# Recurrence of two GRU layers: the half-precision state cast on ScalarE, candidate sums in PSUM, keep's high products last

## The chip, the cores and the metric

The kernel runs on one core of a Trainium2 chip. The metric is the time of one execution on the device in microseconds (us), median of three runs. A core has five engines that matter here, each with its own queue worked off in order: TensorE (PE; its weight loads are listed as PEld), VectorE (DVE), ScalarE (ACT), GpSimd (POOL) and SyncE (SP, which issues DMAs). They meet only through semaphores.

## The reference

Four layers over x of shape (8, 16, 16, 96): a spectral block, a Toeplitz block, and two blocks that are the same function with other weights. Each of those two normalises x, projects it, and runs four GRUs over the 256 positions (two directions for each of two weight sets), then gates and projects back. What matters is the GRU step:

```python
def step(hprev, gxt):
    gh = hprev @ whh.T + bhh
    r = jax.nn.sigmoid(gxt[:, :h] + gh[:, :h])
    z = jax.nn.sigmoid(gxt[:, h:2 * h] + gh[:, h:2 * h])
    n = jnp.tanh(gxt[:, 2 * h:] + r * gh[:, 2 * h:])
    hn = (1.0 - z) * n + z * hprev
    return (hn, hn)
```

The batch is 8 and h is 96. The 256 steps of a layer can't be reordered, as each takes the state of the step before.

## The kernel before

The program runs the layers one after the other. `gru_steps` holds the recurrence of one layer and is called twice (tensor names L2s_... and L3s_...). The four GRUs are two groups of two: group g handles its two GRUs with 8 batch rows each, PER = 16 columns on 96 partitions. The groups don't depend on each other. Every engine's queue treats group 0, then group 1, of step q, then goes on to q + 1, so while one group waits for an engine the other can use it.

The state is kept in fp32 (`states`, all 257 of them), and for the products as two half-precision parts: `h_hi`, the state rounded, and `h_lo`, what is left. Weights are in two half-precision parts too. In PSUM lie the sums of three gates, 8 steps (STEPS) to a chunk and two chunks deep: reset and keep (r and z) and cand (n). The input's share is added ahead of time by products of 64 columns (8 rows by 8 steps, L1161) for the next chunk, `ahead(gate, first)`: six for each gate and group, spread over the steps from `first` on. The hidden state's share (L1185, 8 columns each) is per group and step: for each gate four "high" products (two weight parts, two GRUs) with h_hi, and two "low" ones with h_lo. Sums of a chunk that was used are zeroed by ScalarE (L1135, L1137) at two steps of a chunk.

One step of a group, engine by engine:

- TensorE waits for h_hi (L1193), adds the high products of reset, cand and keep, then input products for reset, waits for h_lo (L1205), adds low reset (releases the reset sigmoid), low cand, input products for keep, low keep (releases the keep sigmoid), input products for cand.
- ScalarE: reset sigmoid (L1128), keep sigmoid (L1130), renew = sigmoid of the negated keep sum (L1131), then tanh of the candidate (L1133).
- VectorE: `candidate` (L1063), `kept_part` (L1070, keep times old state), `new_state` and `rest` (L1085, h_lo = state - h_hi). Multiply-and-add of two tensors is done by a scan over interleaved pairs of 32 elements for 16 results: with pairs (0, a) and (k, b) it gives k * a + b at the odd places. `new_state` issues the scan twice: once with half-precision output into h_hi (L1077), once in fp32 into `states` (L1079).

VectorE's order over both groups is written out by hand:

```python
candidate(0, q); rest(1, q - 1); kept_part(0, q); new_state(0, q)
candidate(1, q); rest(0, q);     kept_part(1, q); new_state(1, q)
```

(two lines here for eight in the kernel). From the middle of a layer on GpSimd adds forward and backward states into `y` (L1112), four operations each time 8 steps are complete.

Of the kernel before, what the change touches and what calls it, by code (L numbers as in the profile page):

```python
# [27 lines left out]
ALU = mybir.AluOpType  # L28
ACT = mybir.ActivationFunctionType

P = 128
BATCH, SIDE, C = 8, 16, 96
# [35 lines left out]
PER = 2 * BATCH  # L68


def flat(ap):

    return ap.rearrange("p a b -> p (a b)")
# [921 lines left out]
def gru_steps(nc, layer, weights, forward, states, y):  # L995
# [8 lines left out]
    with ExitStack() as ctx:  # L1004
# [3 lines left out]
        each = lambda n: [sem(f"{n}{g}") for g in range(GROUPS)]  # L1008
        bank = lambda n: ctx.enter_context(nc.psum_tensor(f"{layer}s_{n}", [P, 4, PER, STEPS], F32))
        reset = pairs("reset", [C, 2, PER, 2])  # L1010
        cand = pairs("cand", [C, 2, PER, 2])
        keep = pairs("keep", [C, 2, PER])
        renew = pairs("renew", [C, 2, PER, 2])
        terms = pairs("terms", [C, 2, PER, 2])
# [7 lines left out]
        reset_sum = lambda g, p: reset_bank[g][:, p]  # L1022
        keep_sum = lambda g, p: keep_bank[g][:, p]
        cand_sum = lambda g, p: cand_bank[g][p][:, 0:2].rearrange("p a c s -> p (a c) s").rearrange("p (c k) s -> p c k s", k=2)
        warm = sb("warm", [C, 1])
        prepared = sem("prepared")

# [10 lines left out]
        with nc.Block() as block:  # L1038

            @block.vector  # L1040
            def _(e):
# [16 lines left out]
                def candidate(g, q):  # L1058

                    p, s = q // STEPS % 2, q % STEPS  # L1060
                    x = q % 2
                    e.wait_ge(advanced[g], 5 * q + 2)
                    e.tensor_tensor_scan(flat(cand[g][:, x]), flat(reset[g][:, x]), flat(cand_sum(g, p)[0:C, :, :, s]), 0.0,  # L1063
                                         ALU.mult, ALU.add).then_inc(cand_ready[g], 1)

                def kept_part(g, q):
# [6 lines left out]
                def new_state(g, q):  # L1073

                    x = q % 2
                    e.wait_ge(advanced[g], 5 * q + 5)
                    e.tensor_tensor_scan(flat(h_hi[g][0:C, x]), flat(renew[g][:, x]), flat(terms[g][:, x]), 0.0,  # L1077
                                         ALU.mult, ALU.add).then_inc(hi_ready[g], 1)
                    e.tensor_tensor_scan(flat(states[g][:, q + 1]), flat(renew[g][:, x]), flat(terms[g][:, x]), 0.0,  # L1079
                                         ALU.mult, ALU.add).then_inc(updated[g], 1)  # L1080

                def rest(g, q):

                    e.wait_ge(updated[g], q + 1 + BEFORE[g])
                    e.tensor_tensor(h_lo[g][:, q % 2], states[g][:, q + 1, :, 1], h_hi[g][0:C, q % 2, :, 1],  # L1085
                                    ALU.subtract).then_inc(lo_ready[g], 1)

# [27 lines left out]
            @block.scalar  # L1115
            def _(e):

                e.wait_ge(prepared, 1)
                e.activation(warm[:], warm[:], ACT.Sigmoid)
                e.wait_ge(prepared, PREPARED)  # L1120
                for q in range(SEQ):
                    p, s = q // STEPS % 2, q % STEPS
                    x = q % 2
                    renewed = 1 <= q // STEPS < CHUNK_COUNT - 1
                    for g in range(GROUPS):

                        e.wait_ge(reset_summed[g], q + 1)
                        e.activation(reset[g][:, x, :, 1], reset_sum(g, p)[0:C, :, s], ACT.Sigmoid).then_inc(advanced[g], 1)  # L1128
                        e.wait_ge(keep_summed[g], q + 1)
                        e.activation(keep[g][:, x], keep_sum(g, p)[0:C, :, s], ACT.Sigmoid).then_inc(advanced[g], 1)  # L1130
                        e.activation(renew[g][:, x, :, 1], keep_sum(g, p)[0:C, :, s], ACT.Sigmoid, scale=-1.0)  # L1131
                        e.wait_ge(cand_ready[g], q + 1)
                        e.activation(terms[g][:, x, :, 0], cand[g][:, x, :, 1], ACT.Tanh).then_inc(advanced[g], 1)  # L1133
                        if renewed and s == RESET_ZEROED:
                            e.activation(reset_sum(g, 1 - p)[0:C], zeros[:], ACT.Copy).then_inc(zeroed[g], 1)  # L1135
                        if renewed and s == KEEP_ZEROED:
                            e.activation(keep_sum(g, 1 - p)[0:C], zeros[:], ACT.Copy).then_inc(zeroed[g], 1)  # L1137

            @block.tensor
            def _(e):  # L1140
# [34 lines left out]
                for q in range(SEQ):  # L1175
# [3 lines left out]
                    for g in range(GROUPS):  # L1179
# [14 lines left out]

                        before, at = divmod(q - 1, STEPS)
                        zeroing = 1 <= before < CHUNK_COUNT - 1 and at in (RESET_ZEROED, KEEP_ZEROED)
                        for gate in (CAND, KEEP, RESET) if zeroing and at == RESET_ZEROED else (RESET, CAND, KEEP):
                            if zeroing and gate == (RESET if at == RESET_ZEROED else KEEP):
                                e.wait_ge(zeroed[g], 2 * (before - 1) + (1 if at == RESET_ZEROED else 2))
                            for j in range(2):  # L1200
                                add(gate, 0, 0, j)
                                add(gate, 1, 0, j)
                        ahead(RESET, RESET_ZEROED + 1)

                        e.wait_ge(lo_ready[g], q + 1)  # L1205
# [1 line left out]
                        add(RESET, 0, 1, 1).then_inc(reset_summed[g], 1)  # L1207
                        add(CAND, 0, 1, 0)
                        add(CAND, 0, 1, 1).then_inc(advanced[g], 1)
                        ahead(KEEP, KEEP_ZEROED + 1)  # L1210
                        add(KEEP, 0, 1, 0)
                        add(KEEP, 0, 1, 1).then_inc(keep_summed[g], 1)
# [186 lines left out]
```

## Time and profile before

| | |
|---|---|
| median of 3 runs | 1206.0 us (1205.65 to 1208.2) |
| the profiled execution | 1204.91 us |
| its span in the profile | 1203.1 us |
| busy TensorE / VectorE / ScalarE / GpSimd | 1085.8 / 950.9 / 773.5 / 154.9 us |
| granted TensorE clock, mean | 0.583 of full speed |
| DMA over the span | 12.59 MB |

Times of rows are from the start of the span. A matmul's end is modelled, so its start is what tells; a group of alike matmuls in a row is shown as one line with the start of the first. The time of an instruction that follows directly on another overlaps it.

### The profile page before, as it was taken

What the parts mean: (1) busy time and instruction counts of PE and PEld (TensorE: products, weight loads), DVE (VectorE), ACT (ScalarE), POOL (GpSimd) and SP (SyncE); (2) the same over time, 40 slices, a digit from 0 to 9 for tenths busy, and PEclk for the clock granted to TensorE, in tenths of its full rate; (3) what the DMA queues carried; (4) which work ended last, traced back from release to release, by engine and by line L of the source; (5) the groups of instructions that cost most, each with busy time, mean ns of one, the idle gap of its engine ahead of it and who ended that gap; (6) DMA issues with size and microseconds to landing.
All of it is one profiled execution on the core that took longest, in us unless ns stands there. A gap on an engine that the chain in (4) does not pass through costs nothing. (4 is left out here: it accounts for less than half of the span.)

```text
span 1203.1 us, 55551 instructions
## 1 busy us (share of the span) xinstructions
PE 1085.8 (90%) x22424; PEld 860.0 (71%) x22424; DVE 950.9 (79%) x5703; ACT 773.5 (64%) x4503; POOL 154.9 (13%) x222
## 2 busy tenths in 40 slices
PE   3787799958999999999999989999999999999997
PEld 2554344445888888888888866788888888888886
DVE  3544699987888888888888876788888888888884
ACT  4223530007788788777777773788788777777773
POOL 1001379920000000001000100000000001000100
PEclk9587899957555555555555556555555555555555
DMA  4000500000000000000000000000000000000000
GB/s 121 2 1 12 133 1 1 1 0 7 4 4 4 4 4 4 4 4 4 4 4 4 3 4 5 4 4 3 4 4 4 4 3 4 4 4 4 4 4 27
DMA packets 8220, 12.59 MB, mean 10 GB/s; under 512 B 5746, under 2 KB 7122, under 8 KB 7675
## 3 DMA queue, kind: packets, MB, share of 16 engines
q1 hardware_dynamic: 7962, 9.05, 3.0%
q8 instruction: 175, 2.87, 1.0%
q14 instruction: 83, 0.67, 0.2%
HBM read 8.26 MB, written 0.79 MB: 8 GB/s over the span
## 5 line engine op out<-in xcount | busy, mean ns | idle before, releaser
L1077 DVE TENSOR_TENSOR_SCAN L3s_h_hi<-L3s_renew,L3s_terms 96x32 f16<-96x32 f32 x512 | 114.5, 224 | 64.3
L1077 DVE TENSOR_TENSOR_SCAN L2s_h_hi<-L2s_renew,L2s_terms 96x32 f16<-96x32 f32 x512 | 114.5, 224 | 64.2
L1185 PE MATMUL L3s_reset_sum<-L3s_h_hi,L_w_hidden 97*128 97x8 f16 x2048 | 139.6, 179 | 11.6 <-DVEq L1054 0.4
L1185 PE MATMUL L2s_reset_sum<-L2s_h_hi,L_w_hidden 97*128 97x8 f16 x2048 | 139.6, 179 | 11.6 <-DVEq L1054 0.4
L1112 POOL TENSOR_TENSOR L_y<-L_states 96x64 f32<-96x64 f32 x128 | 40.9, 355 | 843.1 <-DVE L_states L1079 843.1
L1185 PEld LDWEIGHTS L3s_reset_sum<-L3s_h_hi,L_w_hidden 97*128 97x128 f16 x2048 | 94.4, 107 | 62.1 <-DVE L3s_h_hi L1077 13.8
L1185 PEld LDWEIGHTS L2s_reset_sum<-L2s_h_hi,L_w_hidden 97*128 97x128 f16 x2048 | 94.4, 107 | 62.1 <-DVE L2s_h_hi L1077 13.8
L1133 ACT ACTIVATE L3s_terms<-L3s_cand 96x16 f32<-96x16 f32 x512 | 111.5, 218 | 37.5 <-DVE L3s_cand L1063 6.0
L1133 ACT ACTIVATE L2s_terms<-L2s_cand 96x16 f32<-96x16 f32 x512 | 111.5, 218 | 37.4 <-DVE L2s_cand L1063 5.9
L1185 PE MATMUL L3s_cand_sum<-L3s_h_hi,L_w_hidden 97*128 97x8 f16 x2048 | 131.3, 175 | 4.5 <-DVE L3s_h_hi L1077 3.1
L1185 PE MATMUL L2s_cand_sum<-L2s_h_hi,L_w_hidden 97*128 97x8 f16 x2048 | 131.3, 175 | 4.5 <-DVE L2s_h_hi L1077 3.1
L1185 PE MATMUL L3s_keep_sum<-L3s_h_hi,L_w_hidden 97*128 97x8 f16 x2048 | 130.0, 174 | 0.0
L1185 PE MATMUL L2s_keep_sum<-L2s_h_hi,L_w_hidden 97*128 97x8 f16 x2048 | 130.0, 174 | 0.0
L1128 ACT ACTIVATE L3s_reset<-L3s_reset_sum 96x16 f32<-96x16 f32 x512 | 93.0, 182 | 53.2 <-PE L3s_reset_sum L1185 1.1
L1128 ACT ACTIVATE L2s_reset<-L2s_reset_sum 96x16 f32<-96x16 f32 x512 | 93.0, 182 | 53.2 <-PE L2s_reset_sum L1185 1.0
L1185 PE MATMUL L3s_reset_sum<-L3s_h_lo,L_w_hidden 96*128 96x8 f16 x1024 | 114.1, 185 | 0.5 <-DVE L3s_h_lo L1085 0.2
L1185 PE MATMUL L2s_reset_sum<-L2s_h_lo,L_w_hidden 96*128 96x8 f16 x1024 | 114.0, 185 | 0.4 <-DVE L2s_h_lo L1085 0.2
L1185 PE MATMUL L3s_keep_sum<-L3s_h_lo,L_w_hidden 96*128 96x8 f16 x1024 | 112.1, 183 | 0.0
L1185 PE MATMUL L2s_keep_sum<-L2s_h_lo,L_w_hidden 96*128 96x8 f16 x1024 | 112.1, 183 | 0.0
L1063 DVE TENSOR_TENSOR_SCAN L3s_cand<-L3s_reset,L3s_cand_sum 96x32 f32<-96x32 f32 x512 | 110.4, 216 | 2.0 <-ACT L3s_reset L1128 1.1
L1063 DVE TENSOR_TENSOR_SCAN L2s_cand<-L2s_reset,L2s_cand_sum 96x32 f32<-96x32 f32 x512 | 110.4, 216 | 2.0 <-ACT L2s_reset L1128 1.1
L692 DVE SCALAR_TENSOR_TENSOR l_acc<-l_v,coef,l_acc 96x384 f32<-96x384 f32 (+11 forms) x88 | 103.6, 1241 | 0.4
(257 smaller groups left out, 3517.9 us busy)
## 6 DMA issues: line engine op xcount, KB each, us to landing
L_wih_raw<-in_L_wih SPq DMA_DIRECT2D x2, 1152.0 KB, 11.4
l_w_raw<-in_L_w SPq DMA_DIRECT2D x1, 1296.0 KB
L_w_hidden_raw<-in_L_whh SPq DMA_DIRECT2D x2, 576.0 KB
stream<-in_x SPq DMA_DIRECT2D x2, 384.0 KB, 3.8
out<-stream SPq DMA_DIRECT2D x4, 192.0 KB, 2.1
l_idft<-in_idft SPq DMA_DIRECT2D x1, 400.0 KB
rpe_lw<-in_rpe_lw SPq DMA_DIRECT2D x1, 384.0 KB
l_dft<-in_dft SPq DMA_DIRECT2D x1, 288.0 KB, 2.9
```

The source lines that it names most:

```text
L692: e.scalar_tensor_tensor(out=row(to, acc), in0=row(of, v), scalar=coef[:, m, axis, at:at + 1], in1=row(to, acc), op0=ALU.mult, op1=ALU.add ...
L1063: e.tensor_tensor_scan(flat(cand[g][:, x]), flat(reset[g][:, x]), flat(cand_sum(g, p)[0:C, :, :, s]), 0.0, ALU.mult, ALU.add).then_inc(can ...
L1077: e.tensor_tensor_scan(flat(h_hi[g][0:C, x]), flat(renew[g][:, x]), flat(terms[g][:, x]), 0.0, ALU.mult, ALU.add).then_inc(hi_ready[g], 1)
L1112: e.tensor_tensor(y[:, m, :, t:t + STEPS].rearrange("p b t -> p t b"), hist[g0][:, t:t + STEPS, j0, :], mirrored, ALU.add)
L1128: e.activation(reset[g][:, x, :, 1], reset_sum(g, p)[0:C, :, s], ACT.Sigmoid).then_inc(advanced[g], 1)
L1133: e.activation(terms[g][:, x, :, 0], cand[g][:, x, :, 1], ACT.Tanh).then_inc(advanced[g], 1)
L1185: return e.matmul(dst, weights.hidden[0:rows, wp, GATES * (2 * g + j) + gate, :], rhs, start=False, stop=False, skip_group_check=True)
```

## The change

ScalarE makes h_hi: a copy of the finished fp32 state with half-precision output, `high_half`, issued between the other group's reset sigmoid and keep sigmoid. VectorE's half-precision scan goes. `rest` now waits for h_hi (`hi_ready`) in place of the state (`updated`). The candidate scan writes its 32 results into unused columns of the bank of its own cand sums in PSUM, where tanh reads them, and no longer into SBUF. On TensorE, keep's four high products move from before the wait for h_lo to after the low products of reset and cand; a wait for a zeroed bank stays with its gate. Number and shape of the products are unchanged.

```diff
--- before.py
+++ after.py
@@ -1008,7 +1008,6 @@
         each = lambda n: [sem(f"{n}{g}") for g in range(GROUPS)]
         bank = lambda n: ctx.enter_context(nc.psum_tensor(f"{layer}s_{n}", [P, 4, PER, STEPS], F32))
         reset = pairs("reset", [C, 2, PER, 2])
-        cand = pairs("cand", [C, 2, PER, 2])
         keep = pairs("keep", [C, 2, PER])
         renew = pairs("renew", [C, 2, PER, 2])
         terms = pairs("terms", [C, 2, PER, 2])
@@ -1022,6 +1021,8 @@
         reset_sum = lambda g, p: reset_bank[g][:, p]
         keep_sum = lambda g, p: keep_bank[g][:, p]
         cand_sum = lambda g, p: cand_bank[g][p][:, 0:2].rearrange("p a c s -> p (a c) s").rearrange("p (c k) s -> p c k s", k=2)
+
+        cand = lambda g, p, x: cand_bank[g][p][0:C, 2].rearrange("p c s -> p (c s)")[:, x * 2 * PER:(x + 1) * 2 * PER]
         warm = sb("warm", [C, 1])
         prepared = sem("prepared")
 
@@ -1060,7 +1061,7 @@
                     p, s = q // STEPS % 2, q % STEPS
                     x = q % 2
                     e.wait_ge(advanced[g], 5 * q + 2)
-                    e.tensor_tensor_scan(flat(cand[g][:, x]), flat(reset[g][:, x]), flat(cand_sum(g, p)[0:C, :, :, s]), 0.0,
+                    e.tensor_tensor_scan(cand(g, p, x), flat(reset[g][:, x]), flat(cand_sum(g, p)[0:C, :, :, s]), 0.0,
                                          ALU.mult, ALU.add).then_inc(cand_ready[g], 1)
 
                 def kept_part(g, q):
@@ -1074,14 +1075,12 @@
 
                     x = q % 2
                     e.wait_ge(advanced[g], 5 * q + 5)
-                    e.tensor_tensor_scan(flat(h_hi[g][0:C, x]), flat(renew[g][:, x]), flat(terms[g][:, x]), 0.0,
-                                         ALU.mult, ALU.add).then_inc(hi_ready[g], 1)
                     e.tensor_tensor_scan(flat(states[g][:, q + 1]), flat(renew[g][:, x]), flat(terms[g][:, x]), 0.0,
                                          ALU.mult, ALU.add).then_inc(updated[g], 1)
 
                 def rest(g, q):
 
-                    e.wait_ge(updated[g], q + 1 + BEFORE[g])
+                    e.wait_ge(hi_ready[g], q + 2)
                     e.tensor_tensor(h_lo[g][:, q % 2], states[g][:, q + 1, :, 1], h_hi[g][0:C, q % 2, :, 1],
                                     ALU.subtract).then_inc(lo_ready[g], 1)
 
@@ -1122,15 +1121,22 @@
                     p, s = q // STEPS % 2, q % STEPS
                     x = q % 2
                     renewed = 1 <= q // STEPS < CHUNK_COUNT - 1
+
+                    def high_half(g, q):
+                        e.wait_ge(updated[g], q + 1 + (0, 1)[g])
+                        e.activation(h_hi[g][0:C, q % 2, :, 1], states[g][:, q + 1, :, 1], ACT.Copy).then_inc(hi_ready[g], 1)
+
                     for g in range(GROUPS):
 
                         e.wait_ge(reset_summed[g], q + 1)
                         e.activation(reset[g][:, x, :, 1], reset_sum(g, p)[0:C, :, s], ACT.Sigmoid).then_inc(advanced[g], 1)
+                        if q + g >= 1:
+                            high_half(1 - g, q - 1 + g)
                         e.wait_ge(keep_summed[g], q + 1)
                         e.activation(keep[g][:, x], keep_sum(g, p)[0:C, :, s], ACT.Sigmoid).then_inc(advanced[g], 1)
                         e.activation(renew[g][:, x, :, 1], keep_sum(g, p)[0:C, :, s], ACT.Sigmoid, scale=-1.0)
                         e.wait_ge(cand_ready[g], q + 1)
-                        e.activation(terms[g][:, x, :, 0], cand[g][:, x, :, 1], ACT.Tanh).then_inc(advanced[g], 1)
+                        e.activation(terms[g][:, x, :, 0], cand(g, p, x).rearrange("p (c k) -> p c k", k=2)[:, :, 1], ACT.Tanh).then_inc(advanced[g], 1)
                         if renewed and s == RESET_ZEROED:
                             e.activation(reset_sum(g, 1 - p)[0:C], zeros[:], ACT.Copy).then_inc(zeroed[g], 1)
                         if renewed and s == KEEP_ZEROED:
@@ -1194,12 +1200,15 @@
 
                         before, at = divmod(q - 1, STEPS)
                         zeroing = 1 <= before < CHUNK_COUNT - 1 and at in (RESET_ZEROED, KEEP_ZEROED)
-                        for gate in (CAND, KEEP, RESET) if zeroing and at == RESET_ZEROED else (RESET, CAND, KEEP):
+                        def high(gate):
                             if zeroing and gate == (RESET if at == RESET_ZEROED else KEEP):
                                 e.wait_ge(zeroed[g], 2 * (before - 1) + (1 if at == RESET_ZEROED else 2))
                             for j in range(2):
                                 add(gate, 0, 0, j)
                                 add(gate, 1, 0, j)
+
+                        for gate in (CAND, RESET) if zeroing and at == RESET_ZEROED else (RESET, CAND):
+                            high(gate)
                         ahead(RESET, RESET_ZEROED + 1)
 
                         e.wait_ge(lo_ready[g], q + 1)
@@ -1207,6 +1216,7 @@
                         add(RESET, 0, 1, 1).then_inc(reset_summed[g], 1)
                         add(CAND, 0, 1, 0)
                         add(CAND, 0, 1, 1).then_inc(advanced[g], 1)
+                        high(KEEP)
                         ahead(KEEP, KEEP_ZEROED + 1)
                         add(KEEP, 0, 1, 0)
                         add(KEEP, 0, 1, 1).then_inc(keep_summed[g], 1)
```

## Rows read from the trace of the kernel before

**Rows 1.** Line 1063, whole run: durations min/median/max, first and last start.
```profile
L1063 DVE TENSOR_TENSOR_SCAN L2s_cand<-L2s_reset,L2s_cand_sum x512: 184/217/217, 292.9 to 714.1; 96x32 f32<-96x32 f32 x171
```

**Rows 2.** The same line between 260 and 375 us.
```profile
L1063 DVE TENSOR_TENSOR_SCAN L2s_cand<-L2s_reset,L2s_cand_sum x101: 216/217/217, 292.9 to 374.2; 96x32 f32<-96x32 f32 x101
```

**Rows 3.** A stretch: five engines' busy time, PEclk, DMA share, GB/s.
```profile
250.00:650.00 400.00, 376.86 (x8966) 316.79 (x8967) 333.73 (x2279) 297.85 (x1871) 15.86 (x45) 0.52 0.02 4
```

**Rows 4.** Timeline of one half: start us, duration us, alike instructions merged.
```profile
500.80 0.22 DVE L1077 TENSOR_TENSOR_SCAN L2s_h_hi<-L2s_renew,L2s_terms 96x32 f16<-96x32 f32 x1
...
501.01 0.18 ACT L1130 ACTIVATE L2s_keep<-L2s_keep_sum 96x16 f32<-96x16 f32 x1
...
501.08 0.28 PE L1185 MATMUL L2s_reset_sum<-L2s_h_hi,L_w_hidden 97*128 97x8 f16 x4
501.09 0.17 ACT L1131 ACTIVATE L2s_renew<-L2s_keep_sum 96x16 f32<-96x16 f32 x1
501.12 0.22 DVE L1063 TENSOR_TENSOR_SCAN L2s_cand<-L2s_reset,L2s_cand_sum 96x32 f32<-96x32 f32 x1
...
501.21 0.25 PE L1185 MATMUL L2s_cand_sum<-L2s_h_hi,L_w_hidden 97*128 97x8 f16 x4
501.25 0.15 DVE L1085 TENSOR_TENSOR L2s_h_lo<-L_states,L2s_h_hi 96x16 f16<-96x16 f32 x1
...
501.32 0.25 PE L1185 MATMUL L2s_keep_sum<-L2s_h_hi,L_w_hidden 97*128 97x8 f16 x4
501.32 0.17 DVE L1070 TENSOR_TENSOR L2s_terms<-L2s_keep,L_states 96x16 f32<-96x16 f32 x1
501.37 0.22 ACT L1133 ACTIVATE L2s_terms<-L2s_cand 96x16 f32<-96x16 f32 x1
...
501.46 0.22 PE L1185 MATMUL L2s_reset_sum<-L2s_h_lo,L_w_hidden 96*128 96x8 f16 x2
501.49 0.26 ACT L1135 ACTIVATE L2s_reset_sum<-L2s_zeros 96x128 f32<-96x128 f32 x1
...
501.53 0.20 PE L1185 MATMUL L2s_cand_sum<-L2s_h_lo,L_w_hidden 96*128 96x8 f16 x2
...
501.62 0.22 DVE L1077 TENSOR_TENSOR_SCAN L2s_h_hi<-L2s_renew,L2s_terms 96x32 f16<-96x32 f32 x1
...
501.71 0.18 ACT L1128 ACTIVATE L2s_reset<-L2s_reset_sum 96x16 f32<-96x16 f32 x1
501.76 0.20 DVE L1079 TENSOR_TENSOR_SCAN L_states<-L2s_renew,L2s_terms 96x32 f32<-96x32 f32 x1
...
501.93 0.22 DVE L1063 TENSOR_TENSOR_SCAN L2s_cand<-L2s_reset,L2s_cand_sum 96x32 f32<-96x32 f32 x1
```

**Rows 5.** Timeline of TensorE in a later step.
```profile
505.65 0.21 PE L1161 MATMUL L2s_keep_sum<-L_forward,L_w_input 97*128 97x64 f16 x1
505.68 0.23 PE L1185 MATMUL L2s_keep_sum<-L2s_h_lo,L_w_hidden 96*128 96x8 f16 x2
505.76 0.21 PE L1161 MATMUL L2s_cand_sum<-L_forward,L_w_input 96*128 96x64 f16 x1
```

**Rows 6.** Groups of ScalarE by shape: busy us, mean ns, idle before.
```profile
L1133 ACT ACTIVATE L2s_terms<-L2s_cand 96x16 f32<-96x16 f32 x512 | 111.5, 218 | 37.4 <-DVE L2s_cand L1063 5.9
...
L1131 ACT ACTIVATE L2s_renew<-L2s_keep_sum 96x16 f32<-96x16 f32 x512 | 88.5, 173 | 0.0
...
L1137 ACT ACTIVATE L2s_keep_sum<-L2s_zeros 96x128 f32<-96x128 f32 x60 | 15.6, 260 | 0.0
...
L927 ACT ACTIVATE L2i_gate_parts<-L2i_w_gate 96x192 f16<-96x192 f32 x1 | 0.4, 362 | 0.8 <-DMA L2i_affine<-in_L_ln 0.8
...
L925 ACT ACTIVATE L2i_minus<-ident 96x96 f16<-96x96 f32 x1 | 0.3, 267 | 0.0
```

**Rows 7.** Timeline while GpSimd adds: VectorE, then GpSimd.
```profile
702.10 0.32 DVE L1077 TENSOR_TENSOR_SCAN L2s_h_hi<-L2s_renew,L2s_terms 96x32 f16<-96x32 f32 x1
...
701.68 1.28 POOL L1112 TENSOR_TENSOR L_y<-L_states 96x64 f32<-96x64 f32 x4 [12.11 <-DVE L_states L1079]
```

## The prediction

> **What bounds the kernel now.** I read the page first (its main numbers are in the table above): the span is 1203.1 us, and its execution took 1204.91 us against a median of 1206.0 us over the three runs shown. That is 1.1 us below, less than the runs differ among themselves, so I add my differences to 1206.0. TensorE is busy for 90% and VectorE for 79%, but those shares are no answer in a recurrence: each engine is often busy with one group while the other group waits. Nearly all the time lies in two stretches that `gru_steps` sets. In the first layer the candidate scan runs 512 times, from 292.9 to 714.1 us, and the second layer's 512 span as much [rows 1]. I call one such unit, one group's step, a half: there are 1024. In a quiet stretch 101 of them begin between 292.9 and 374.2 us, which is 81.3 / 100 = 0.813 us a half [rows 2]. The granted clock there is about half, the 1.2 GHz level, and the change gives TensorE no more work per us, so I leave the clock alone [rows 3].
>
> (Starts in the timeline have two decimals, so one gap is good to 10 ns; the gaps that I give as 32, 33, 57, 137 and 182 are means over neighbouring halves, the durations medians, like the 217 of the candidate scan [rows 2].) Then the timeline of one half [rows 4], following one group from the start of its candidate scan, 501.12. The scan takes 0.217 us, and tanh starts 0.033 later (501.37); 0.218 of tanh and 0.032 later the half-precision scan starts (501.62), the fp32 scan of the same values 0.14 later (501.76), and the other group's candidate scan at 501.93. But that last scan did not wait for the fp32 scan alone: two scans in a row start 0.14 apart and this gap is 0.17. What ended last was the other group's reset sigmoid (501.71 + 0.182 = 501.89). Followed back: reset sigmoid <- low-half products of that group at 501.46 <- its h_lo subtraction at 501.25 <- the candidate scan at 501.12, behind which it is queued on VectorE. In ns: 137 + 146 + 57 + 75 to the second pair (501.53) + 182 + 182 + 32 = 811, a whole half of 813. So the loop goes from one group's candidate scan to the other's, and the tanh is not in it.
>
> A second loop is just as long: the group's own. Scan 217 + 33 + tanh 218 + 32 + half-precision scan 221 + 57 to the first product (501.02 to 501.08) + 130 + 110 + 110 for the twelve high products (501.08, .21, .32) + 54 for two low products of reset + 182 + 182 + 32 = 1578. Where a 64-column input product for the reset gate is slipped in it is longer: such a product costs 0.05 us net, as the one for keep at 505.65 shows (0.03 to the next product, then 0.08 where two products otherwise take 0.054) [rows 5]. So 1628, against 2 x 813 = 1626. Both loops bind at once, which is why a change must shorten both to win.
>
> **The change, part by part.** *Half-precision scan removed, cast on ScalarE added.* h_hi no longer comes straight from the terms but from the finished state. The fp32 scan now starts after a wait, where the other scan took 0.22 instead of the 0.20 that it takes right behind it [rows 4]; I use 220. Then a handover to ScalarE (33, as scan to tanh) and the cast. No row has this cast. Bounds from near rows [rows 6]: 173 for an activation queued behind another (renew, out of PSUM), 218 for tanh, the same 16 columns from SBUF to SBUF. The fp32-to-f16 copies on ScalarE take 362 ns for 192 columns and 267 for 96, so 0.99 a column and 188 at 16 columns. I take 205, about the middle between that and tanh. Handover to TensorE as now from VectorE: 57, with 30 (ScalarE to VectorE) as the lower end. So high products become possible 220 + 33 + 205 + 57 = 515 after the last wait, in place of 221 + 57 = 278: 237 later.
>
> The Trainium skill (ScalarE: Activation LUTs, What ACT_TABLE_LOAD costs) gives 186 ns + 0.833 a column for an activation with immediate scale and bias, so an estimate of 199 for 16 columns; by it the sum below would end some 6 us lower, and this case has only the rows just named beside it.
>
> *Keep's high products last.* Four of twelve products, 110, leave the path in front of the low reset products. Their wait for h_lo disappears too: h_lo is ready 32 + 146 + 57 = 235 after the cast against 57 + 240 = 297 on TensorE, so the second low product follows at 27 instead of 48, already in the 54 that I use. In return the keep sum comes later. After low reset and low cand products come four high keep products, perhaps an input product, and two low ones: keep's sigmoid starts 54 + 107 + 54 = 215 after reset's start, 265 with the input product, where the two follow each other much closer now. The kept part then starts at scan + 1 (or 51) + 180 + 32 = 263 and ends at 430, and with 32 the new state could start at 462. By the tanh it could start at 217 + 33 + 180 + 32 = 462. A dead heat, so I cost it at nothing; any slip of it is paid in full (rival below). The zeroing waits come with the gate that they came with and are a step old.
>
> *Candidate in PSUM.* Tanh now reads PSUM. The sigmoids out of PSUM take 0.18, tanh out of SBUF 218: tanh becomes 180, a gain of 38. What the scan pays for writing PSUM no row shows. Bounds: on ScalarE the 128-column zeroing into PSUM takes 260, where the copies into SBUF give 267 + 32 x 0.99 = 299 for as many columns, 39 less; I take 50 less as one end and 50 more as the other [rows 6]. The scan that already reads PSUM takes 217 and the half-precision scan, all in SBUF, 0.22, so the middle, no change, is nearest [rows 4].
>
> [...]
>
> *The sums.* Own loop: 217 + 33 + 180 + 32 + 220 + 33 + 205 + 57 + 240 + 54 + 182 + 182 + 32 = 1667, and 1717 with an input product for reset. That product comes in 6 of 8 steps (six products over steps 1 to 7), so 1705 on average, 852 a half.
> A new loop appears on ScalarE, since the cast of a group is queued behind the other group's reset sigmoid: cast 205 + 57 + 240 + 54 + 182 to the start of this group's reset sigmoid, then the issue distance to the other group's cast. Between keep and renew that is 80 (501.01, 501.09), between tanh and the zeroing 120 (501.37, 501.49) [rows 4]; a sigmoid of 182 is like the first, so 84. Sum 822, with the input product 872, on average 860 a half. Behind the cast on ScalarE wait keep's and renew's sigmoids, but keep starts 215 or more after reset, later than 84 + 109, so the cast is hidden for them. On VectorE h_lo now waits for the cast, and behind it is queued the kept part: the cast ends 84 + 205 = 289 after the reset sigmoid's start, while h_lo's place in the queue comes at 214 + 137 = 351, so nothing is delayed.
> VectorE loses one scan a half (141 of start distance) and gains nothing from it in quiet halves, as it idles before the new state anyway. Only where GpSimd adds up the output does it pay: there VectorE's operations stretch, the half-precision scan by 0.10 to 0.32 us [rows 7]. That happens once in 8 steps in the back half of each layer, 32 times, so -3 us.
> Result: 860 - 813 = +47 ns x 1024 = +48 us, less 3: 1206 + 45 = 1251 us.
>
> **Rivals.**
> 1. *The cast is cheap.* If it costs 173 like renew, the loops are 1673 / 2 = 836 and 828: +23 x 1024 - 3 = +21, 1227 us. With a handover of 30 to TensorE on top it would be 823, 1213 us. For it: the cast is queued behind a sigmoid. Against: it reads SBUF, and waits.
> 2. *Keep comes too late.* Its chain ties with tanh to the nanosecond. A slip of 50 (one more input product's worth) makes the own loop 1755, 877 a half: +64 x 1024 - 3, 1269 us.
> 3. *Writing PSUM is dear.* 50 more in the scan, own loop 1755 again, 1269 us. If it is 50 cheaper, the keep chain holds the step and nothing is won.
> 4. *VectorE is the bound, and the change is faster.* Place: the scan pair on VectorE. Price: each half loses the 141 between the two scans, 672 a half, 1206 - 144 = 1062 us. It decides if VectorE has no idle time before the new state. Against: in this half it is done with the kept part at 501.32 + 0.17 = 501.49 and idles until 501.62 [rows 4].
> 5. *The cast is hidden and nothing changes*, 1206 us. For that the cast and its handovers must cost 80 ns less on the own loop (1705 - 1626) and 47 less on ScalarE's: a cast of 125 would do both, and no row of ScalarE is that short.
>
> **How the numbers follow.** Forecast 1251, chance 0.54, with its own range of 1238 to 1266 (cast and issue distance off by 12). Rival 1: 0.14. Rival 2: 0.12. Rival 3: 0.09. Rival 4: 0.05, or another gain of that sort. Rival 5: 0.06, split over all three outcomes. The range reaches down to rival 1, most of the way to its cheap handover, and up past 2 and 3: 1215 to 1278 us; an issue distance of 120 would give 896 a half, 1288, and is left out. A measurement of this kernel can tell some 0.2% (2.4 us) from no change. Faster 0.07 (rival 4 and a third of 5), same 0.02, slower 0.91.
>
> **What would show it.** The half becomes 0.85 to 0.87 us and longer in steps with the input product (0.87) than without (0.83), where it is 0.813 now in all. The cast lasts 0.20 to 0.21 and starts either 0.03 after the state scan's end or about 0.08 after the other group's reset sigmoid's start. The first high product starts 0.51 after the state scan does; low reset products follow without a gap. Tanh takes 0.18, the candidate scan 0.22. VectorE's busy time falls by some 200 us in total and its idle time grows by more. I am wrong if the cast is much under 0.17, if the scan into PSUM departs from 0.22 by over 0.05, if keep's sigmoid rather than tanh releases the new state, or if TensorE's granted clock moves.

## The result, and the profile after

The change made the kernel slower: 1252.99 us (median of 4, 1251.72 to 1254.53) against 1205.83 us, a ratio of 1.0391, 95% interval 1.0367 to 1.0415. The forecast was 1251 us.

The page of the changed kernel, engines and clock:

```profile
span 1249.9 us, 55549 instructions
...
PE 1073.2 (86%) x22424; PEld 844.9 (68%) x22424; DVE 906.1 (72%) x4679; ACT 816.0 (65%) x5525; POOL 155.5 (12%) x222
...
PEclk9587899956555555555555557555555555555555
```

VectorE's busy time fell from 950.9 to 906.1 us, ScalarE's rose from 773.5 to 816.0, TensorE is idle for longer (177 us in place of 117), and the granted clock stayed at the 1.2 GHz level through both recurrences (5 tenths in nearly every slice of PEclk). Fewer VectorE instructions (4679 against 5703), a longer kernel.

Line 1064, the candidate scan (L1063 before), over the whole run and up to 381 us: durations min/median/max, first and last start.

```profile
L1064 DVE TENSOR_TENSOR_SCAN L2s_cand_sum<-L2s_reset,L2s_cand_sum x512: 224/225/225, 292.8 to 737.5; 96x32 f32<-96x32 f32 x171
```

```profile
L1064 DVE TENSOR_TENSOR_SCAN L2s_cand_sum<-L2s_reset,L2s_cand_sum x102: 224/225/225, 292.8 to 380.4; 96x32 f32<-96x32 f32 x102
...
  ACT L2s_reset L1132: 16.9, 90
```

As in [rows 2], 87.6 us over 101 intervals: 0.867 us a half, where it was 0.813. That is 54 ns x 1024 = 55 us more. Over all 512 candidate scans it is 444.7 / 511 = 0.870 where [rows 1] give 0.824, so GpSimd's additions cost less than before (0.003 a half in place of 0.011): 8 us back, 47 in all, as measured. VectorE now waits for the reset sigmoid in 90 of the 102 halves.

The timeline of one half, next to [rows 4]:

```profile
503.96 0.22 DVE L1078 TENSOR_TENSOR_SCAN L_states<-L2s_renew,L2s_terms 96x32 f32<-96x32 f32 x1
...
504.15 0.18 ACT L1132 ACTIVATE L2s_reset<-L2s_reset_sum 96x16 f32<-96x16 f32 x1
...
504.23 0.21 ACT L1127 ACTIVATE L2s_h_hi<-L_states 96x16 f16<-96x16 f32 x1
504.36 0.23 DVE L1064 TENSOR_TENSOR_SCAN L2s_cand_sum<-L2s_reset,L2s_cand_sum 96x32 f32<-96x32 f32 x1 [0.18 <-ACT L2s_reset L1132]
504.41 0.18 ACT L1136 ACTIVATE L2s_keep<-L2s_keep_sum 96x16 f32<-96x16 f32 x1
...
504.49 0.28 PE L1191 MATMUL L2s_reset_sum<-L2s_h_hi,L_w_hidden 97*128 97x8 f16 x4
...
504.50 0.16 DVE L1084 TENSOR_TENSOR L2s_h_lo<-L_states,L2s_h_hi 96x16 f16<-96x16 f32 x1
...
504.62 0.18 ACT L1139 ACTIVATE L2s_terms<-L2s_cand_sum 96x16 f32<-96x16 f32 x1
504.62 0.25 PE L1191 MATMUL L2s_cand_sum<-L2s_h_hi,L_w_hidden 97*128 97x8 f16 x4
504.62 0.17 DVE L1071 TENSOR_TENSOR L2s_terms<-L2s_keep,L_states 96x16 f32<-96x16 f32 x1
...
504.73 0.21 PE L1167 MATMUL L2s_reset_sum<-L_forward,L_w_input 97*128 97x64 f16 x1
...
504.76 0.23 PE L1191 MATMUL L2s_reset_sum<-L2s_h_lo,L_w_hidden 96*128 96x8 f16 x2
...
504.83 0.22 DVE L1078 TENSOR_TENSOR_SCAN L_states<-L2s_renew,L2s_terms 96x32 f32<-96x32 f32 x1
...
505.02 0.18 ACT L1132 ACTIVATE L2s_reset<-L2s_reset_sum 96x16 f32<-96x16 f32 x1 [0.22 <-PE L2s_reset_sum L1191]
...
505.10 0.21 ACT L1127 ACTIVATE L2s_h_hi<-L_states 96x16 f16<-96x16 f32 x1
```

Follow ScalarE's queue. The cast (L1127) starts at 504.23, 0.08 behind the other group's reset sigmoid (L1132), and ends at 504.44. TensorE's first high product starts at 504.49; the eight high products of reset and cand and an input product (L1167) follow, then without a gap the low products (504.76); the reset sigmoid at 505.02, and the next cast at 505.10: 0.87 us, a half. The new state's scan started at 504.83 and ended at 505.05, so with 0.034 for the handover this cast could have started at 505.085. Its place in the queue came 10 to 15 ns later. In this half both conditions of the cast are met nearly at the same time.

Durations of the operations in question in a quiet stretch (ns, min/median/max), cast and h_lo, then tanh and state scan:

```profile
L1084 DVE TENSOR_TENSOR L2s_h_lo<-L_states,L2s_h_hi x116: 157/158/172, 300.0 to 399.6; 96x16 f16<-96x16 f32 x116
L1127 ACT ACTIVATE L2s_h_hi<-L_states x115: 209/211/222, 300.5 to 399.4; 96x16 f16<-96x16 f32 x115
```

```profile
L1139 ACT ACTIVATE L2s_terms<-L2s_cand_sum x116: 180/181/183, 300.1 to 399.7; 96x16 f32<-96x16 f32 x116
...
L1078 DVE TENSOR_TENSOR_SCAN L_states<-L2s_renew,L2s_terms x116: 220/221/222, 300.3 to 400.0; 96x32 f32<-96x32 f32 x116
```

### The profile page after: what moved, and what is told of

The parts are those of the page before. It is cut to its first block and busy times, and to the rows that moved or that the text cites. A ratio compares the mean times of both kernels' runs of the same rounds, so it can differ in the third digit from the quotient of the medians.

```text
span 1249.9 us, 55549 instructions
## 1 busy us (share of the span) xinstructions
PE 1073.2 (86%) x22424; PEld 844.9 (68%) x22424; DVE 906.1 (72%) x4679; ACT 816.0 (65%) x5525; POOL 155.5 (12%) x222
## 5 line engine op out<-in xcount | busy, mean ns | idle before, releaser
L1064 DVE TENSOR_TENSOR_SCAN L2s_cand_sum<-L2s_reset,L2s_cand_sum 96x32 f32<-96x32 f32 x512 | 115.1, 225 | 88.7 <-ACT L2s_reset L1132 77.8
L1064 DVE TENSOR_TENSOR_SCAN L3s_cand_sum<-L3s_reset,L3s_cand_sum 96x32 f32<-96x32 f32 x512 | 115.1, 225 | 88.7 <-ACT L3s_reset L1132 77.5
L1132 ACT ACTIVATE L3s_reset<-L3s_reset_sum 96x16 f32<-96x16 f32 x512 | 92.5, 181 | 92.0 <-PE L3s_reset_sum L1191 83.9
L1132 ACT ACTIVATE L2s_reset<-L2s_reset_sum 96x16 f32<-96x16 f32 x512 | 92.5, 181 | 91.9 <-PE L2s_reset_sum L1191 83.9
L1078 DVE TENSOR_TENSOR_SCAN L_states<-L3s_renew,L3s_terms 96x32 f32<-96x32 f32 x512 | 113.8, 222 | 23.2
L1078 DVE TENSOR_TENSOR_SCAN L_states<-L2s_renew,L2s_terms 96x32 f32<-96x32 f32 x512 | 113.8, 222 | 23.1
L1127 ACT ACTIVATE L2s_h_hi<-L_states 96x16 f16<-96x16 f32 x511 | 108.7, 213 | 0.0
L1127 ACT ACTIVATE L3s_h_hi<-L_states 96x16 f16<-96x16 f32 x511 | 108.7, 213 | 0.0
L1191 PEld LDWEIGHTS L3s_cand_sum<-L3s_h_hi,L_w_hidden 97*128 97x128 f16 x2048 | 94.3, 104 | 14.5 <-ACT L3s_h_hi L1127 14.5
```

Source lines behind the costliest of these rows:

```text
L1064: e.tensor_tensor_scan(cand(g, p, x), flat(reset[g][:, x]), flat(cand_sum(g, p)[0:C, :, :, s]), 0.0, ALU.mult, ALU.add).then_inc(cand_read ...
L1127: e.activation(h_hi[g][0:C, q % 2, :, 1], states[g][:, q + 1, :, 1], ACT.Copy).then_inc(hi_ready[g], 1)
L1191: return e.matmul(dst, weights.hidden[0:rows, wp, GATES * (2 * g + j) + gate, :], rhs, start=False, stop=False, skip_group_check=True)
```

## The experiments

The theory: two kinds of loop set the time. One is a group's own, passed once in two halves, the other goes through an engine's queue from group to group and is passed in every half: VectorE's in the kernel before (candidate scan, the other group's h_lo, low products, reset sigmoid), ScalarE's in the changed one (cast, products, reset sigmoid, the other group's cast). The rivals: only the own loop counts; the cast is hidden; VectorE's load counts. Each kernel was timed against the kernel before on the same chip. That kernel's median there was 1204.87 to 1206.39 us, so times from different chips can be compared to about 1.5 us.

**The cast alone** (cast_only). The candidate stays in SBUF and keep's high products stay in front of the wait.

```diff
-                    e.tensor_tensor_scan(flat(h_hi[g][0:C, x]), flat(renew[g][:, x]), flat(terms[g][:, x]), 0.0,
-                                         ALU.mult, ALU.add).then_inc(hi_ready[g], 1)
...
+                        if q + g >= 1:
+                            high_half(1 - g, q - 1 + g)
```

> Only the cast on ScalarE is taken over; the candidate stays in SBUF and keep's high products stay in front of the wait for h_lo. Theory (two loops, the cast of one group queued behind the other's reset sigmoid): ScalarE's loop is 210 + 55 + 350 + 54 + 182 + 80 = 931 a half, 982 with an input product for reset, 969 on average, which exceeds the own loop (1859 / 2 = 930). So 0.97 us a half and about 1359 us. Rival, only a group's own loop counts: 930 a half, about 1318 us. Rival, the cast is hidden: 1206 us.

Measured: 1350.71 us, ratio 1.1194 (1.1167 to 1.1222). ScalarE's timeline (reset sigmoid and cast, then the next cast):

```profile
504.96 0.18 ACT L1131 ACTIVATE L2s_reset<-L2s_reset_sum 96x16 f32<-96x16 f32 x1 [0.24 <-PE L2s_reset_sum L1190]
505.04 0.21 ACT L1126 ACTIVATE L2s_h_hi<-L_states 96x16 f16<-96x16 f32 x1
...
506.02 0.21 ACT L1126 ACTIVATE L2s_h_hi<-L_states 96x16 f16<-96x16 f32 x1
```

From cast to cast 0.98, with the forecast 982 for a step with an input product. Over a quiet stretch the half is 0.965, forecast 969. The own loop alone would have given 930 and 1318 us; that rival is out. The cast and its handovers cost 145 us when nothing else pays for them.

**The candidate sums in PSUM alone** (psum_only).

```diff
-                    e.tensor_tensor_scan(flat(cand[g][:, x]), flat(reset[g][:, x]), flat(cand_sum(g, p)[0:C, :, :, s]), 0.0,
+                    e.tensor_tensor_scan(cand(g, p, x), flat(reset[g][:, x]), flat(cand_sum(g, p)[0:C, :, :, s]), 0.0,
```

> Only the candidate sums go to PSUM. Theory: the loop over VectorE's queue (candidate scan, the other group's h_lo, low products, reset sigmoid) still sets 813 a half and tanh is not in it, so nothing is won; if a longer scan into PSUM (225 in place of 217) also puts off the h_lo behind it by 8, 821 a half. 1206 to 1214 us. Rival, the group's own loop alone sets the time: 1628 - 30 = 1598, 799 a half, 1191 us.

Measured: 1217.61 us, ratio 1.0097 (1.0074 to 1.012): slower by 11.7 us, 4 us above what was expected. The scan takes 225, but what stands behind it takes longer too, h_lo with 158 in place of 146 (this kernel, then the kernel before):

```profile
L1085 DVE TENSOR_TENSOR L2s_h_lo<-L_states,L2s_h_hi x145: 156/158/159, 300.2 to 419.2; 96x16 f16<-96x16 f32 x145
```

```profile
L1085 DVE TENSOR_TENSOR L2s_h_lo<-L_states,L2s_h_hi x148: 144/146/148, 300.4 to 419.9; 96x16 f16<-96x16 f32 x148
```

The half grew to 0.83 (505.08 to 505.91; 0.826 on average between 300 and 420 us), and from the candidate scan's start to h_lo's start it is as before (505.08 to 505.22, where 501.12 to 501.25 stands in [rows 4]):

```profile
505.08 0.23 DVE L1063 TENSOR_TENSOR_SCAN L2s_cand_sum<-L2s_reset,L2s_cand_sum 96x32 f32<-96x32 f32 x1
505.22 0.16 DVE L1085 TENSOR_TENSOR L2s_h_lo<-L_states,L2s_h_hi 96x16 f16<-96x16 f32 x1
...
505.91 0.22 DVE L1063 TENSOR_TENSOR_SCAN L2s_cand_sum<-L2s_reset,L2s_cand_sum 96x32 f32<-96x32 f32 x1
```

So it is h_lo's 12 ns, not the scan's 8, that VectorE's loop pays. Tanh's gain of 37 is worth nothing here. The rival with only the own loop (1191 us) is out: this loop exists and tanh is not in it.

**Keep's products last alone** (keep_only), and **both without the cast** (psum_keep).

```diff
-                        for gate in (CAND, KEEP, RESET) if zeroing and at == RESET_ZEROED else (RESET, CAND, KEEP):
+                        for gate in (CAND, RESET) if zeroing and at == RESET_ZEROED else (RESET, CAND):
...
+                        high(KEEP)
                         ahead(KEEP, KEEP_ZEROED + 1)
```

> Only keep's high products are moved behind the low products of reset and cand. Theory: VectorE's queue still sets 813 a half, keep's sigmoid comes later but before tanh is due (462 against 501 after the candidate scan's start), so 1206 us, give or take 3. Rival, the own loop alone: 1628 - 110 = 1518, 759 a half, 1151 us. Rival, keep now comes too late: up to 50 a turn, 1230 us.

> The change without its cast: both of the parts that shorten the own loop, with the half-precision scan kept. Theory: the own loop falls to about 1490, 745 a half, but VectorE's queue holds 813 to 821, so 1206 to 1214 us. Rival, the own loop alone sets the time: 1135 us and a kernel that beats both.

Measured: keep_only 1207.63 us, ratio 1.001 (0.9996 to 1.0025), no difference that can be told; psum_keep 1218.57 us, ratio 1.0108 (1.0085 to 1.0131), which lies 5 us above its range for the reason just shown, h_lo's 12 ns. The own loop is now shorter by 110 or 140 ns and nothing is gained: VectorE's queue holds the time. In the kernel before both parts are worthless without the cast.

**The cast with keep last, the candidate in SBUF** (cast_keep): cast_only and keep_only together.

> The change with the candidate left in SBUF. Theory: tanh reads SBUF again (218), the candidate scan is back to 217, so the own loop is 1721 + 30 = 1751 on average, 876 a half, and now exceeds ScalarE's loop (859): about +9 ns a half on 867, 1262 us. Rival, keep's sigmoid and not tanh releases the new state in the change: the later tanh is then covered, 1253 us. Rival, the same cost as in the kernel without the cast (PSUM costs 12 us there): 1241 us.

Measured: 1265.06 us, ratio 1.05 (1.0484 to 1.0516), 3 us over the forecast. So the parts are worth this, in us over the kernel before: cast alone +145, with keep last +60, with the candidate in PSUM too +47. Keep last is worth 85 us where the cast has put the high products on a loop that is passed in every half, and nothing before; PSUM is worth 12 us there and costs 12 before. Keep's later sigmoid, with its tie in the sum, did not cover tanh's gain: that rival's 1253 us is out.

**One more copy in ScalarE's queue** (extra_copy) and **the cast in front of the sigmoid** (cast_first), both from the changed kernel.

```diff
+                        e.activation(spare_copy[:, (2 * q + g) % 8], zeros[:, :, 0], ACT.Copy)
                         if q + g >= 1:
                             high_half(1 - g, q - 1 + g)
```

```diff
-                        e.activation(reset[g][:, x, :, 1], reset_sum(g, p)[0:C, :, s], ACT.Sigmoid).then_inc(advanced[g], 1)
                         if q + g >= 1:
                             high_half(1 - g, q - 1 + g)
+                        e.wait_ge(reset_summed[g], q + 1)
+                        e.activation(reset[g][:, x, :, 1], reset_sum(g, p)[0:C, :, s], ACT.Sigmoid).then_inc(advanced[g], 1)
```

> The changed kernel with one more copy of 16 columns on ScalarE between each reset sigmoid and the cast behind it; it reads zeros, writes a spare tensor and nothing waits for it. Theory (ScalarE's queue is a loop that is passed in every half): the issue distance of a copy, 115 ns, is paid in every half, about 980 a half, 1369 us. Rival, ScalarE has room (it is busy for 65%) and the cast waits for the state rather than for its place: 1253 to 1265 us. Rival, only the own loop counts, paid once in two halves: 58 a half, 1312 us.

> The changed kernel with the cast placed before the other group's reset sigmoid in ScalarE's queue in place of behind it. Theory: the reset sigmoid then waits for the cast, and a new loop joins both groups: cast 115 to the sigmoid, 181 + 32 + 225 + 34 + 181 + 34 + 221 + 34 to the next cast, 1057 a half, 1448 us. Rival, the order of two short operations matters only by their length: 1253 us, or some us less since the cast starts 12 ns sooner.

Measured: extra_copy 1361.75 us, ratio 1.1307 (1.1286 to 1.1328), 109 us for a copy that nobody waits for, on an engine that was busy for 65%. Its queue on ScalarE:

```profile
504.93 0.18 ACT L1133 ACTIVATE L2s_reset<-L2s_reset_sum 96x16 f32<-96x16 f32 x1 [0.33 <-PE L2s_reset_sum L1193]
505.01 0.22 ACT L1134 ACTIVATE L2s_spare_copy<-L2s_zeros 96x16 f16<-96x16 f32 x1
505.13 0.21 ACT L1128 ACTIVATE L2s_h_hi<-L_states 96x16 f16<-96x16 f32 x1
```

The cast starts 0.20 behind the sigmoid's start in place of 0.08. The half is 0.976 (980 forecast). The 109 lie near the 116 of a loop passed in every half and far from the 59 of the own loop. cast_first 1433.64 us, ratio 1.1912 (1.1886 to 1.1937), 14 us under its forecast:

```profile
505.65 0.22 ACT L1127 ACTIVATE L2s_h_hi<-L_states 96x16 f16<-96x16 f32 x1 [0.29 <-DVE L_states L1078]
505.77 0.16 ACT L1134 ACTIVATE L2s_reset<-L2s_reset_sum 96x16 f32<-96x16 f32 x1
...
506.69 0.22 ACT L1127 ACTIVATE L2s_h_hi<-L_states 96x16 f16<-96x16 f32 x1 [0.29 <-DVE L_states L1078]
```

The sigmoid directly behind the cast takes 0.16, not the 0.18 that I had used, and starts 0.12 behind it; 1.04 from cast to cast, 1.057 forecast. The order is worth 181 us: where the cast stands in ScalarE's queue is a choice between two loops, and the change had the better one.

**Reset's input products ahead of the wait** (inputs_early), from the changed kernel, for steps 2 to 7.

```diff
+                        if s > RESET_ZEROED + 1:
+                            ahead(RESET, RESET_ZEROED + 1)
                         e.wait_ge(hi_ready[g], q + 1)
...
-                        ahead(RESET, RESET_ZEROED + 1)
+                        if s <= RESET_ZEROED + 1:
+                            ahead(RESET, RESET_ZEROED + 1)
```

> The changed kernel with reset's input products of steps 2 to 7 issued before the wait for h_hi, where TensorE idles, in place of behind the high products. Theory: the 50 ns of such a product leave both loops, own 1683 / 2 = 842 and ScalarE's 821, as in the one half of eight that takes 826 now; 842 to 846 a half, about 1231 us. Rival, the product isn't on the path but TensorE's total work is: 1253 us.

Measured: 1235.46 us, ratio 1.0253 (1.0233 to 1.0272), 17 us under the changed kernel with the same products in another place. The half is 0.851, 5 to 9 ns over the forecast: VectorE's timeline shows candidate scans 0.83 and 0.87 apart in turn.

```profile
505.53 0.23 DVE L1064 TENSOR_TENSOR_SCAN L2s_cand_sum<-L2s_reset,L2s_cand_sum 96x32 f32<-96x32 f32 x1 [0.17 <-ACT L2s_reset L1132]
...
506.36 0.23 DVE L1064 TENSOR_TENSOR_SCAN L2s_cand_sum<-L2s_reset,L2s_cand_sum 96x32 f32<-96x32 f32 x1
...
507.23 0.22 DVE L1064 TENSOR_TENSOR_SCAN L2s_cand_sum<-L2s_reset,L2s_cand_sum 96x32 f32<-96x32 f32 x1 [0.17 <-ACT L2s_reset L1132]
```

Two halves are 1.70, which is the own loop: 1667, 8 more for the scan at 225, and up to 17 for the cast, which takes 222 where it waits for the state rather than for its place. ScalarE's loop is now the shorter one. So the 0.05 us of an input product was on both loops, and the sum of the own loop was some 25 ns short.

**Without GpSimd's additions** (no_adds_before, no_adds_after).

```diff
-                for q in range(SEQ // 2, SEQ, STEPS):
...
+                e.memset(y[:], 0.0)
```

> The kernel before without GpSimd's additions of forward and backward states: y is set to zero instead, so the output is not the reference's. Theory: the halves hit by the additions (1136 and 862 in place of 813, 15 times in each layer inside the loop) fall back to 813, 372 ns x 30 = 11.2 us, and the four additions behind each layer's last step, 1.3 us twice, go too: 1191 us. Rival, the additions are covered: 1205 us.

> The changed kernel without GpSimd's additions; y is set to zero instead, so the output is not the reference's. Theory: the additions cost the changed kernel less, 53 and 79 ns in the two halves that they hit and little after them, about 122 ns x 30 = 3.7 us, since one scan less stands in their way and ScalarE's loop has slack on VectorE; with the 2.6 us behind the layers 1247 us. The difference to the kernel before without additions would then be 56 us, 53.3 ns x 1024 and a little. Rival, the additions cost both kernels alike and the step alone grew by 47 us: 1239 us.

Measured: 1191.57 us, ratio 0.9881 (0.9851 to 0.9911), and 1245.67 us, ratio 1.033 (1.0302 to 1.0358). The difference of the two is 54 us, which is the growth of 54 ns in 1024 halves (55 us) by itself. The additions cost 14.8 us before and 7.3 after. VectorE's timeline while they run (724.65 to 725.95) in the changed kernel, next to [rows 7]:

```profile
724.64 0.23 DVE L1064 TENSOR_TENSOR_SCAN L2s_cand_sum<-L2s_reset,L2s_cand_sum 96x32 f32<-96x32 f32 x1
...
725.15 0.27 DVE L1078 TENSOR_TENSOR_SCAN L_states<-L2s_renew,L2s_terms 96x32 f32<-96x32 f32 x1
725.56 0.23 DVE L1064 TENSOR_TENSOR_SCAN L2s_cand_sum<-L2s_reset,L2s_cand_sum 96x32 f32<-96x32 f32 x1
725.70 0.28 DVE L1084 TENSOR_TENSOR L2s_h_lo<-L_states,L2s_h_hi 96x16 f16<-96x16 f32 x1
...
726.51 0.23 DVE L1064 TENSOR_TENSOR_SCAN L2s_cand_sum<-L2s_reset,L2s_cand_sum 96x32 f32<-96x32 f32 x1 [0.19 <-ACT L2s_reset L1132]
```

h_lo takes up to 0.28, the state scan 0.27; from candidate scan to candidate scan it is 0.92 and 0.95, so 0.13 more than two quiet halves, where the same pair was 1.14 and 0.86 in the kernel before (expectation above), 0.37 more. My 3 us counted only the removed scan's own stretch.

**A version from this** (rest_gpsimd, rest_gpsimd_psum). The kernel before loses by h_lo standing behind the candidate scan in VectorE's queue. GpSimd can subtract in its place:

```diff
-                    rest(1, q - 1)
...
-                    rest(0, q)
...
+                        e.wait_ge(updated[g], q + 1 + (0, 1)[g])
+                        if q + 1 < SEQ:
+                            e.tensor_tensor(h_lo[g][:, q % 2], states[g][:, q + 1, :, 1], h_hi[g][0:C, q % 2, :, 1],
+                                            ALU.subtract).then_inc(lo_ready[g], 1)
+                        if due:
+                            add(*due.pop(0))
```

The diff is on GpSimd from the third part on; `due` holds the four additions of y after each 8 steps. Both have keep last, the second also the candidate in PSUM, and h_hi comes from VectorE's scan.

> The kernel before with keep's high products last, and h_lo's subtraction moved from VectorE to GpSimd, whose additions are spread one behind each subtraction. It breaks the loop over VectorE's queue that sets 813 a half. Theory: what is left is VectorE's order through tanh and the two scans, 501 + 141 + 141 = 783, and the own loop, 502 + 336 + 35 + the subtraction + 57 + 48 + 212 + 214; with 250 for the subtraction (the 64-column additions take 355) 1654, 827 a half, 1217 us; with 160 it would be 783 and 1172 us. Rival, GpSimd at work stretches VectorE's operations in every half as its additions do now in one of 16 (0.17 to 0.34, 0.22 to 0.32): 100 to 300 ns a half more, 1310 us and over.

> The same with the candidate sums in PSUM, too. Theory: without h_lo behind it on VectorE the longer h_lo after a scan into PSUM (158 in place of 146) no longer counts, while tanh out of PSUM saves 37 and the scan costs 8: 29 less on the own loop and on VectorE's order, 15 to 29 ns a half below rest_gpsimd, so 15 to 30 us less than it. Rival, writing PSUM costs here as it did in psum_only: 12 us more than it.

Measured: rest_gpsimd 1218.15 us, ratio 1.0103 (1.0083 to 1.0123), slower by 12 us as forecast, with halves of 0.831. rest_gpsimd_psum 1200.66 us, ratio 0.9959 (0.9938 to 0.9979), 17.5 us less: 0.4% faster than the kernel before and 4% faster than the changed one. Its candidate scans up to 400 us and over the whole run:

```profile
L1063 DVE TENSOR_TENSOR_SCAN L2s_cand_sum<-L2s_reset,L2s_cand_sum x132: 197/225/225, 292.7 to 399.6; 96x32 f32<-96x32 f32 x132
```

```profile
L1063 DVE TENSOR_TENSOR_SCAN L2s_cand_sum<-L2s_reset,L2s_cand_sum x512: 197/225/225, 292.7 to 712.8; 96x32 f32<-96x32 f32 x171
```

The quiet half is 106.9 / 131 = 0.816, which is 3 ns more than in the kernel before (0.813 [rows 2]); only over all 512 it is less, 0.822 against 0.824 [rows 1]. So the 0.4% does not come from the loops. The trace puts it to GpSimd's additions, which this kernel spreads one behind each subtraction: they lengthen the mean half by 0.006 in place of 0.011, which makes the mean 2 ns shorter (2 us in all), and from the last candidate scan to the end of the span it takes 22.3 us in place of 24.5. Spreading the additions alone, in the kernel before, was not run.

The subtraction on GpSimd and the kept part on VectorE in a quiet stretch, and the timeline of both engines around one half:

```profile
L1108 POOL TENSOR_TENSOR L2s_h_lo<-L_states,L2s_h_hi x147: 213/214/217, 300.1 to 419.3; 96x16 f16<-96x16 f32 x147
```

```profile
L1070 DVE TENSOR_TENSOR L2s_terms<-L2s_keep,L_states x147: 171/172/216, 300.2 to 419.5; 96x16 f32<-96x16 f32 x147
```

```profile
505.63 0.20 DVE L1079 TENSOR_TENSOR_SCAN L_states<-L2s_renew,L2s_terms 96x32 f32<-96x32 f32 x1
...
505.91 0.21 POOL L1108 TENSOR_TENSOR L2s_h_lo<-L_states,L2s_h_hi 96x16 f16<-96x16 f32 x1 [0.68 <-DVE L_states L1079]
...
506.02 0.17 DVE L1070 TENSOR_TENSOR L2s_terms<-L2s_keep,L_states 96x16 f32<-96x16 f32 x1
...
506.18 0.22 PE L1188 MATMUL L2s_reset_sum<-L2s_h_lo,L_w_hidden 96*128 96x8 f16 x2
```

The state scan ends at 505.83, the subtraction runs from 505.91 to 506.12, the low products start at 506.18; VectorE's kept part beside it takes 0.17 as ever, so the feared stretch of every half did not come. The same PSUM that cost 12 us in psum_only is worth 17 here: h_lo has left the queue behind the scan, and the half fell by 15 ns (0.831 to 0.816), half of the 29 by which the own loop became shorter. By that, what binds now is the own loop, with the subtraction on GpSimd in it.

## Why the prediction was right

*The two loops of the kernel before.* VectorE's loop is shown: keep_only and psum_keep shortened the own loop by 110 and 140 ns and gained nothing, and psum_only paid just for the operation in VectorE's loop that became longer. That the own loop was as long rests on the sum (1628 against 1626) alone: no run shortens VectorE's loop and leaves the own one as it was. The versions with h_lo on GpSimd break VectorE's loop but put the subtraction into the own one, and their quiet halves, 0.831 and 0.816, are no shorter than 0.813.

*The cast.* Forecast 205, measured 210 behind the sigmoid (bounds 173 and 218) and 222, above the upper bound, where it waits for the state. Handover to TensorE (504.44 to 504.49) as forecast. High products were possible 504.49 - 503.96 = 0.53 after the start of that state scan, 0.515 in the sum: the cast's 5 more, and some 10 for its place in the queue.

*ScalarE's loop* was the term that made the forecast, 860 a half; the trace shows 867. Where the 7 come from, three candidate scans and a cast of the changed kernel show, a little behind the timeline above:

```profile
506.98 0.23 DVE L1064 TENSOR_TENSOR_SCAN L2s_cand_sum<-L2s_reset,L2s_cand_sum 96x32 f32<-96x32 f32 x1 [0.18 <-ACT L2s_reset L1132]
...
507.59 0.18 ACT L1132 ACTIVATE L2s_reset<-L2s_reset_sum 96x16 f32<-96x16 f32 x1 [0.17 <-PE L2s_reset_sum L1191]
...
507.71 0.22 ACT L1127 ACTIVATE L2s_h_hi<-L_states 96x16 f16<-96x16 f32 x1
...
507.81 0.23 DVE L1064 TENSOR_TENSOR_SCAN L2s_cand_sum<-L2s_reset,L2s_cand_sum 96x32 f32<-96x32 f32 x1
...
508.67 0.23 DVE L1064 TENSOR_TENSOR_SCAN L2s_cand_sum<-L2s_reset,L2s_cand_sum 96x32 f32<-96x32 f32 x1 [0.17 <-ACT L2s_reset L1132]
```

These are two halves without an input product for reset, as two of every eight are. They take 0.83 and 0.87, 1.69 together. That is not ScalarE's loop (forecast 822 each, 1644), it is the own loop: 1667 + 8 for the scan + 17 for the cast = 1692, the same as in inputs_early. The cast at 507.71 starts 0.12 behind the sigmoid and not 0.08, so it waited for the state. The other six halves share 8 x 0.867 - 1.69, which is 0.874 each; there ScalarE's loop holds, forecast 872 (the cast is 5 longer, its place 4 sooner). So 6 of the 7 come from the halves without the product and 1 from the others. Part of that was to be had from the prediction's own numbers: it averaged each loop over the steps and then took the longer one, 860, where step by step the own loop is the longer of the two without the product (1667 against 1644). Its sign "0.83 without the product" came true for every other one of these halves only.

*Keep's high products last:* low products without a gap, keep's sigmoid 0.26 behind reset's (504.15, 504.41), 265 forecast. The tie with tanh held: tanh ended at 504.80 and the state scan started at 504.83, with the kept part done at 504.79. Rival 2 did not occur.

*The candidate in PSUM.* Tanh 181 (180 forecast), scan 225 (217 taken, 167 to 267 as bounds). What no term had was the operation behind the scan: h_lo 158 in place of 146. In the changed kernel it had slack and cost nothing; in psum_only it was nearly all of the loss (12 of the 13 ns a half). The Trainium skill (VectorE: DVE Perf Modes, The TRN2 errata) gives VectorE 120 cycles in place of 58 where the source lies in PSUM. The trace does not agree at 32 elements: the candidate scan, with one source in PSUM, took 217 ns, and the half-precision scan, all in SBUF, 221.

*The mis-sized term:* GpSimd's additions, -3 us forecast, -7.5 measured by the two kernels without them (14.8 and 7.3). Against it stand 7 us too little in the halves (54 ns in place of 47, x 1024). So it is in part luck that 1251 was forecast and 1253 measured: two errors, +7 and -4.5 us, nearly cancel.

*VectorE as the bound* (rival 4) is out by the changed kernel itself: 45 us less busy time on it, and a longer kernel. The prediction had put that fall at some 200 us, which is wrong; it is about a whole scan in each of 1024 halves, as if nothing had overlapped. The two scans started 0.14 apart and together took 0.336, the remaining one takes 0.222: 114 ns less. Most of that comes back, since operations that overlapped now stand apart. The kept part starts 0.12 behind h_lo (504.50, 504.62) in place of 0.07, and the candidate scan no longer starts before the state scan in front of it has ended. Between 300 and 400 us VectorE was busy for 83.9 us before and 74.8 after, which is 0.682 and 0.648 in a half: 34 ns less.

## What to carry to other kernels

In a recurrence with two independent groups on in-order queues, list each group's own loop and also each loop that passes from group to group through a queue, for an operation in the second kind costs twice as much. Compare them step by step, not by their averages; an engine that is 65% busy can be the bound, and a copy that nobody waits for can cost 9%. A loop that binds hides what another loop gains: test a part alone and it is worth nothing, or 85 us, by what else is changed. Before moving work to the idler engine, add its handover and its full latency to the loop. When a version is faster, look whether its quiet half is shorter too: here it was not, and the gain lay elsewhere.

## What the runs showed of the hardware

- A 16-column operation on VectorE right behind a scan that writes PSUM took 158 ns, 146 behind one that writes SBUF (psum_only against the kernel before, all else alike), and 172 where it waited for the cast (extra_copy). The scan itself took 225 against 217.
- An activation's duration depends on its place: the reset sigmoid took 0.18 after a wait and 0.16 right behind the cast (cast_first), the cast 210 behind a sigmoid and 222 where it waited.
- GpSimd's additions of 64 columns stretched VectorE's operations beside them (the half-precision scan to 0.32 us from 0.22 [rows 7], h_lo to 0.28 from 0.16 in the changed kernel); its subtractions of 16 columns, 214 ns each in every half, mostly did not: VectorE's kept part stayed at 0.172 in the median, with 0.216 as the most in the quiet stretch. In the whole of rest_gpsimd_psum the kept part takes 0.20 to 0.24 beside a subtraction only where that starts at most 40 ns before it, and up to 0.35 beside a spread addition. So timing is a part of that difference; what size and layout do stays open.
